# Filled stacks handed to two cross-attention layers, and keys projected ahead of queries

## The reference

```
q = split_heads(layernorm(x) @ w_q + b_q)        # 8 batches, 256 queries, 16 heads of 8
k = split_heads(ctx @ w_k + b_k)                 # 512 keys; ctx is 8 x 512 x 128
v = split_heads(ctx @ w_v + b_v)
scores = einsum('bhqd,bhkd->bhqk', q, k) / sqrt(8)
scores = where(mask == 0, -inf, scores)          # L3x only
x = x + merge(softmax(scores) @ v) @ w_o + b_o   # biases in L1x and L3x only
```

## Time and profile before

| | |
|---|---|
| median of 3 runs | 2776.68 us (2775.05 to 2780.43) |
| the profiled execution | 2782.93 us |
| its span | 2781.1 us, 48541 instructions |
| TensorE busy | 2335.9 us (84%) |
| VectorE busy | 1546.6 us (56%) |
| ScalarE busy | 1362.9 us (49%) |
| GpSimd busy | 728.6 us (26%) |
| mean granted clock of TensorE | 0.921 of 2.4 GHz |

### The profile page before, as it was taken

How to read it: one execution, slowest core, us unless ns; L and a number is a source line. 1 busy time by engine, 2 the same in 40 slices (tenths; PEclk the granted TensorE clock), 3 DMA queues, 4 the chain that set the end, 5 groups by cost and what they waited for, 6 DMA issues and landing times. The chain is left out here.

```text
span 2781.1 us, 48541 instructions
## 1 busy us (share of the span) xinstructions
PE 2335.9 (84%) x16549; PEld 1490.2 (54%) x16595; DVE 1546.6 (56%) x4593; ACT 1362.9 (49%) x3631; POOL 728.6 (26%) x1007
## 2 busy tenths in 40 slices
PE   6969998778898499953759999876969998799989
PEld 4634444745555144431646766555947776366653
DVE  4757772146666677733026666462447776677730
ACT  3736662135554266644217677431326655455542
POOL 0123212444434323102542232114421111322100
PEclk9979999979999699976779999997979999899999
DMA  2023225120000233230440000243520000332200
GB/s 78 2 77 94 86 61 177 37 76 31 25 23 16 57 101 93 65 97 15 93 85 1 2 2 1 80 90 104 162 72 2 1 2 11 99 81 82 61 18 15
DMA packets 129748, 158.29 MB, mean 57 GB/s; under 512 B 23121, under 2 KB 92122, under 8 KB 128355
## 3 DMA queue, kind: packets, MB, share of 16 engines
q1 hardware_dynamic: 117220, 143.47, 18.1%
q0 software_dynamic: 9664, 10.41, 1.8%
q10 hardware_dynamic: 2624, 1.32, 0.3%
HBM read 119.28 MB, written 36.56 MB: 56 GB/s over the span
## 5 line engine op out<-in xcount | busy, mean ns | idle before, releaser
L542 ACT ACTIVATE L3x_p_ring<-L3x_ps_t 128x512 f32<-128x512 f32 x256 | 142.0, 598 | 114.6 <-PE L3x_ps_t L622 113.8
L438 DVE CUSTOM_DVE_ANT_0 L3x_ps_s<-L3x_ps_s,L3x_mask_q 128x512 f32<-128x512 f32 x256 | 169.9, 718 | 38.1 <-PE L3x_ps_s L601 37.0
L542 ACT ACTIVATE L1x_p_ring<-L1x_ps_t 128x512 f32<-128x512 f32 x256 | 140.5, 619 | 87.7 <-PE L1x_ps_t L620 87.7
L441 DVE TENSOR_REDUCE L0x_mx<-L0x_ps_s 128x2 f32<-128x1024 f32 x128 | 152.3, 1221 | 40.3 <-PE L0x_ps_s L601 39.1
L542 ACT ACTIVATE L0x_p_ring<-L0x_ps_t 128x512 f32<-128x512 f32 x256 | 140.8, 622 | 66.8 <-PE L0x_ps_t L620 66.8
L441 DVE TENSOR_REDUCE L1x_mx<-L1x_ps_s 128x2 f32<-128x1024 f32 x128 | 152.2, 1221 | 30.5 <-PE L1x_ps_s L601 29.5
L965 ACT ACTIVATE L2a_probs<-L2a_ps_s,L2a_top 128x256 f32<-128x256 f32 x256 | 117.8, 472 | 78.9 <-DVE L2a_top L915 78.9
L965 ACT ACTIVATE L3a_probs<-L3a_ps_s,L3a_top 128x128 f32<-128x128 f32 (+1 forms) x256 | 104.0, 422 | 39.3 <-DVE L3a_top L911 37.2
L620 PE MATMUL L3x_ps_t<-L3x_q_stack,L3x_k_stack 128*128 128x256 bf16 x512 | 120.6, 275 | 2.7 <-DMA L3x_q_stack<-L3x_m_rows 2.4
L622 PE MATMUL L3x_ps_t<-L3x_mask_k,const_ident_bf 128*128 128x256 bf16 x512 | 119.9, 273 | 0.0
L620 PE MATMUL L0x_ps_t<-L0x_q_stack,L0x_k_stack 128*128 128x256 bf16 x512 | 86.4, 278 | 9.3 <-DMA L0x_q_stack<-L0x_m_rows 3.8
(11 more groups left out here) (718 smaller groups left out, 6204.9 us busy)
## 6 DMA issues: line engine op xcount, KB each, us to landing
L2f_w_e<-L2f_in_w_e SPq DMA_DIRECT2D x23, 544.0 KB
L0x_k_stack<-L0x_k_dram SPq DMA_DIRECT2D x96, 96.0 KB
L1x_k_stack<-L1x_k_dram SPq DMA_DIRECT2D x96, 96.0 KB
L3x_k_stack<-L3x_k_dram SPq DMA_DIRECT2D x96, 96.0 KB
L0f_w<-L0f_in_w SPq DMA_DIRECT2D x32, 256.0 KB, 5.3
L1a_rk_wide<-L1a_rk_dram SPq DMA_DIRECT2D x8, 1024.0 KB, 4.7
L1f_w<-L1f_in_w SPq DMA_DIRECT2D x32, 256.0 KB
kept_x<-ctxT SPq DMA_DIRECT2D x24, 256.0 KB, 3.7
```

Of the source, the lines that this page charges most:

```text
L438: last = dve.tensor_tensor_reduce(span, span, mask_q[:, t, :], 1.0, 2 * MASKED, ALU.add, ALU.max, accum_out=mx[:, t, k:k + 1])
L441: last = dve.tensor_reduce(mx[:, :, k], s_bank(o), AX, ALU.max)
L542: act.activation(p_ring[:, u % RING, j * BANK:(j + 1) * BANK], t_bank(o), ACT.Exp, scale=scale).then_inc(out["t"].sem, 1)
```

## The change

The constants that no layer reads are gone, and the one that `keep_clock` reads has 4 rows instead of 16. For L0x and L3x the stacks are tiles of the surrounding program: GpSimd fills them whole with four memsets, in the first block for L0x and at `x` of batch 2 in L3a for L3x. L1x still has stacks of its own, which ScalarE fills in another order. In all three layers keys come ahead of queries: `k` and the key split move from -13 to -17 (slot 15, two turns before the batch's own), the split is two steps, and the first keys are split by VectorE, the first queries by GpSimd, which clears `v` after that. SyncE stores keys at -17 and queries at -14, loads each quarter's keys ahead of its queries, and leaves the queries of batch 0 to ScalarE's queue. The context load at `ln` (-19) stays where it was.

```
+def fill_stacks(pool, stacks, filled):
+    for n, word in (("k", ONE_PAIR), ("q", 0.0)):
+        for par in range(2):
+            pool.memset(stacks[n][:, par].rearrange("p h k -> p (h k)").bitcast(F32), word).then_inc(filled, 1)
...
-    for kind, k, time, phase in (("ln", 0, -19, 1), ("ln_rest", 0, -18, 1), ("x", 0, -16, 3), ("q", 0, -14, 2), ("k", 0, -13, 2),
-                                 ("split", 0, -13, 3), ("stack", 0, -7, 3), ("stack", 1, -6, 3), ("stack", 2, -5, 3),
+    for kind, k, time, phase in (("ln", 0, -19, 1), ("ln_rest", 0, -18, 1), ("k", 0, -17, 2), ("split_k", 0, -17, 3), ("x", 0, -16, 3),
+                                 ("q", 0, -14, 2), ("split_q", 0, -14, 3), ("stack", 0, -7, 3), ("stack", 1, -6, 3), ("stack", 2, -5, 3),
...
+        def load_stack(eng, name, quarter, b):
+            heads = slice(QUARTER * quarter, QUARTER * (quarter + 1))
+            stack, dram, stored, count = (q_stack, q_dram, q_stored, 32) if name == "q" else (k_stack, k_dram, k_stored, 16)
+            wait_tally(eng, stored, b, count)
+            for a in range(3):
+                rows = dram[a:a + 3] if name == "q" else dram[:]
+                eng.dma_start(stack[24 * a:24 * a + 24, b % 2, heads], rows.rearrange("i (d h) k -> (i d) h k", h=H)[:, heads]
+                              ).then_inc(stacked[quarter].sem, 16)
...
             def _(sp):
-                    if kind == "split":
+                    if kind == "split_k":
+                        wait_tally(sp, k_split, b, 4)
+                        sp.dma_start(k_dram[:].rearrange("i p k -> p i k"), parts["k"][:]).then_inc(k_stored.sem, 16)
+                    if kind == "split_q":
                         wait_tally(sp, q_split, b, 4)
...
-                        elif k == 0:
-                            sp.wait_ge(filled, 2 * (b + 1))
+                        elif clear_own and k == 0:
+                            sp.wait_ge(filled, 1 if b == 0 else 4)
+                        load_stack(sp, "k", k, b)
+                        if b > 0:
+                            load_stack(sp, "q", k, b)
...
             def _(pool):
-                            pool.memset(v[:], 1.0).then_inc(cleared, 1)
...
-                    if kind == "split":
+                    if kind == "split_k" and b > 0:
                         for quarter in stacked:
                             wait_tally(pool, quarter, b, 0)
                         wait_out(pool, ("k", 0, b))
                         split(pool, "k", k_split, b)
+                    if kind == "split_q":
+                        for quarter in stacked:
+                            wait_tally(pool, quarter, b, 0)
+                        wait_out(pool, ("q", 0, b))
+                        split(pool, "q", q_split, b)
+                        if b == 0:
+                            pool.memset(v[:], 1.0).then_inc(cleared, 1)
...
             def _(act):
+                if clear_own:
+                    act.wait_ge(two_made, 1)
+                    fill("k", 0)
...
+                    if kind == "split_q" and b == 0 and clear_own:
+                        fill("q", 0)
+                    if kind == "stack" and b == 0:
+                        if clear_own and k == 0:
+                            act.wait_ge(filled, 2)
+                        load_stack(act, "q", k, b)
+                        if clear_own and k == QUARTER - 1:
+                            fill("k", 1)
+                            fill("q", 1)
...
 def attention_rows(...):
             def _(pool):
+                    if kind == "x" and b == 2 and stacks is not None:
+                        fill_stacks(pool, stacks, filled)
...
 def keep_clock(pe, const, bank, times):
-    wide = const["max_rows"][:, 0:4, :].rearrange("p a k -> p (a k)")
+    wide = const["some_rows"][:].rearrange("p a k -> p (a k)")
...
 def load_constants(nc, const, x_sb, x, const_in, follow, stacks):
+            @block.gpsimd
+            def _(pool):
+                fill_stacks(pool, stacks, filled)
...
-BF16_CONSTS=('ident_bf','causal_min','max_rows','causal_q','causal_k','expert_rows','before','ones_bf')
+BF16_CONSTS=('ident_bf','causal_min','some_rows','expert_rows','before','ones_bf')
```

More of the change, by code:

```diff
@@ L490, in _, with fill @@
             def _(act):
[L491 to L498, removed]
+                def fill(name, par):
+                    rows = stacks[name][P // 2:P, par].rearrange("p h k -> p (h k)").bitcast(F32)
+                    words = two_ones if name == "k" else const["zero"]
+                    act.activation(rows, words[P // 2:P, 0:1].broadcast_to(list(rows.shape)), ACT.Copy).then_inc(filled, 1)
+                if clear_own:
+                    act.wait_ge(two_made, 1)
+                    fill("k", 0)
                 for o in order:
@@ L521, in _ @@
                         wait_tally(act, k_split, b, 0)
+                        if b == 0:
+                            ahead.loaded(act)
                         if qk_bias:
@@ L658, in attention_cross, with attention_rows @@
         sem.clear()
-def attention_rows(nc, x_sb, const, w, cfg, ahead, follow):
+def attention_rows(nc, x_sb, const, w, cfg, ahead, follow, stacks):
     C, kd = cfg["chunks"], cfg["kd"]
@@ L3372, in attention_fidelity_layer, with load_constants @@
         fidelity_tail(nc, x_sb, y_all, const, tail, name + "tail_")
-def load_constants(nc, ctx, x_sb, x, const_in, follow):
-    const = {n: ctx.enter_context(nc.sbuf_tensor("const_" + n, list(a.shape), BF16 if n in BF16_CONSTS else F32))
-             for n, a in const_in.items()}
+def load_constants(nc, const, x_sb, x, const_in, follow, stacks):
     with ExitStack() as own:
         sem = Semaphores(nc, own, "start_")
-        loaded, rounded = sem("loaded"), sem("rounded")
+        loaded, rounded, filled = sem("loaded"), sem("rounded"), sem("filled")
         wide = {n: own.enter_context(nc.sbuf_tensor("wide_" + n, list(const_in[n].shape), F32)) for n in BF16_CONSTS}
@@ L3426, in decoder @@
                 ahead[name].own = False
-        const = load_constants(nc, ctx, x_sb, x, const_in, follow.get("constants"))
+        const = {n: ctx.enter_context(nc.sbuf_tensor("const_" + n, list(a.shape), BF16 if n in BF16_CONSTS else F32))
+                 for n, a in const_in.items()}
+        room, stacks = ExitStack(), {}
+        stacks["L0x"] = cross_stacks(nc, room, "L0x_")
+        load_constants(nc, const, x_sb, x, const_in, follow.get("constants"), stacks["L0x"])
         pool_dma = lambda n: ctx.enter_context(nc.semaphore(n))
@@ L3440, in decoder @@
             elif name in ROWS:
-                attention_rows(nc, x_sb, const, layers[name], dict(ROWS[name], name=name + "_"), ahead[name], follow.get(name))
-            else:
-                attention_cross(nc, x_sb, const, layers[name], dict(ATTENTIONS[name], name=name + "_"), ahead[name])
+                if name == "L3a":
+                    stacks["L3x"] = cross_stacks(nc, room, "L3x_")
+                attention_rows(nc, x_sb, const, layers[name], dict(ROWS[name], name=name + "_"), ahead[name], follow.get(name),
+                               stacks.get("L3x") if name == "L3a" else None)
+            else:
+                attention_cross(nc, x_sb, const, layers[name], dict(ATTENTIONS[name], name=name + "_"), ahead[name], stacks.get(name))
+                room.close()
         if ORDER[-1] == "L3f":
@@ L3462, in consts @@
     c['minus_half']=np.full((128,16),-0.5,np.float32)
-    c['head_rows']=(i[:,None]//8==np.arange(16)[None]).astype(np.float32)
-    mr=np.zeros((128,16,128),np.float32)
+    some_rows=np.zeros((128,4,128),np.float32)
     for p in range(3):
[L3466 to L3470, removed]
+        for h in range(4): some_rows[16*p+h,h]=1
+    c['some_rows']=some_rows
+    later=np.where(i[None,:]>i[:,None],np.float32(1e30),np.float32(0))
+    c['causal_min']=np.concatenate([np.zeros((128,128),np.float32),later],1)
     c['rank_down']=np.broadcast_to((32-np.arange(32)).astype(np.float32),(128,32)).copy()
```

56 lines of the change are left out of this document (20 added, 36 removed).

## The result

The changed kernel took 2837.09 us (median of 5 runs, 2833.02 to 2842.55) against 2775.74 of the kernel before on the same chip: a ratio of 1.0218, 95% interval 1.0201 to 1.0236. It is slower by 61 us. The profiled execution took 2836.67 us (span 2834.5), 53.7 more than that of the kernel before (2782.93, which lay above its median).

What follows compares the result with a forecast made beforehand. TensorE's program order was taken to bound the steady part. Gains -19.5, fill +8.5, waits +38 and clock +9 gave +36 us: 2818.9 against the profiled execution, 2812.7 against the median; range 2782 to 2843.

Steps and rivals of the forecast that it cites:

- Constants: Before the first layer: about 0.9 MB less to load, taken as -2 us, at most 4.4 us gained.
- Starts of L0x, L1x, L3x: Cross layers' starts: earlier key stores and first scores; -8.5 us in L0x, -2 in L1x, -7 in L3x.
- The sentence about query loads: Start of L0x: twelve key loads issued ahead would delay query loads by perhaps 2 us, making the part worth -6.5.
- Fill in L3a: At x of batch 2, GpSimd's memsets delay VectorE's xn and TensorE: +8.5 us (4.4 to 13), half clock included.
- Waits of the key matmul: Cross layers from batch 2 on: the key matmul waits for the late context load, 18 waits, +38 us.
- Half clock: After waits over 2 us TensorE runs at half clock: +9 us at half of ten waits, 0 to 17.
- Keys ahead of queries: Cross layers: the key matmul moves to slot 15 of the turn before and waits for the context tile: +38 us.
- the first (free waits): Cross layers: slack in the batch absorbs TensorE's wait, sum -11 us, 2765.7 us; chance 0.10.
- The second (maxima rows behind the key store): L0x and L1x: maxima's rows wait behind SyncE's key store, 1.6 us in 12 batches, +19, 2785 us; chance 0.08.

Runs made afterwards that it cites:

- the two runs: Queries first, spread fill, filler matmuls ahead of the wait for clearing v: first batch's query loads on ScalarE's queue, 2759.5 us; on SyncE's, 2760.8 us.
- The spread fill: The changed kernel with L3a's four memsets put singly into GpSimd's longest gaps instead of in a row: 2820.4 us.
- the early load: The changed kernel with SyncE issuing the context load at -27 instead of -19, ahead of maxima rows and stack loads: 2791.8 us, ratio 1.0057.
- The held split: The changed kernel with the context load issued early, and GpSimd's key split also waiting for VectorE's maxima parts of batch b-2: 2781.1 us, ratio 1.0019.
- the rows ahead of the stacks: Keys first with early context load, held key split, spread fill, earlier filler, query loads on SyncE, maxima rows issued before next batch's stack loads: 2778.6 us, ratio 1.0009.

## Why the prediction was right, and where it was not

Direction and mechanism hold; 2837.1 lies in the range, 24 us above the forecast. The sum was made against the profiled execution of before, so its terms are compared there: +36 forecast, +53.7 measured.

- *Constants*: -2 forecast, -2.4 measured (first layer begins at 21.6 instead of 24.0).
- *Starts of L0x, L1x, L3x*: -8.5, -2 and -7 forecast; by first `t` against the layer's start -7.2, -4.0 and -7.9. The sum is near (-17.5 and -19.1), the way there was not: first scores in L0x gained 2.1 us, not 6.2, since filler matmuls behind the clearing of `v`, and the query loads with them, took the rest (with both out of the way they came 6.8 earlier than before, 14.2 us after the start); the way from there to first `t` gained 5.2, not 2.3. The sentence about query loads held up 2 us behind the key loads was near the mark: 2.4 to 3.4. The Trainium skill (DMA: Bandwidth & Descriptors, Rules for kernel authors) has all issuing engines share the same 16 DMA engines, so that a second one brings no bandwidth; the two runs agree (143 GB/s with two, from 163 to 168 us, and 170 with one, from 160 to 165). Here the second queue even cost time; whether by itself, or because the key loads of later quarters no longer stood behind the first queries, was not told apart.
- *Fill in L3a*: +8.5 forecast, +11.9 measured. This term was mis-sized: memsets and the two halves of `xn` were taken to alternate (6.5 us). The first half took 10.33 us, the second ended with it, and all four memsets passed: TensorE idled for 9.3, near the bound of 10, and 2.7 went to the half clock, where 2 had been taken. The spread fill shows that the place made the price.
- *Waits of the key matmul*: +38 in 18 forecast, +35.9 in 17 measured; the early load takes them to none. SyncE's queue was the cause, as stated.
- *Half clock*: +9 forecast; from first `t` to the layer's end, busy time times one minus the granted clock grew by 5.9 in L0x and 3.2 in L1x and fell by 0.3 in L3x, in all 8.8.
- *What was missing*: +14.3, the waits for the maxima's parts. The step that failed is the part "Keys ahead of queries", which moves the key matmul and prices only its wait. GpSimd's split moves with it, to the moment when VectorE makes the parts. The earlier trace rows had shown a VectorE instruction held by a memset, and the prediction used this for the fill alone. The held split shows the cause. Of this the Trainium skill (SBUF — State Buffer, Who interferes with whom) says that a VectorE instruction with two SBUF inputs contends with a GpSimd instruction that reads SBUF; the trace agrees (1.13 us instead of 0.17).
- *The rest*: the terms add up to +49.4; the other +4.3 lies spread over steps that were not told apart, and is less than an untouched layer moves from run to run (L1a, above).

Of the rivals, the first (free waits) is out: from first `t` to the end L0x grew by 28.8 us, and its waits and half clock account for some 27, so a batch gave nothing back. The second (maxima rows behind the key store) was rightly priced at nothing while the key matmul waits; once that wait is gone it costs 6 us more than in the changed kernel, and 27 with the rows ahead of the stacks (29.0 in all against 2.1). The median rose by 61 us, the profiled execution by 53.7, because the profiled execution of before lay 7 us above the median of these runs (2775.74) and that of after at its own.

## What to carry to other kernels

When a step is moved forward, list what it needs and where each need's issue stands in its queue, and list what every engine does at the new moment: here the load that had not moved cost some 45 us and the split that had moved with it another 11. Background work on GpSimd has a price that depends on what VectorE is about to do, so put each piece behind an instruction that starts a long gap, not in front of a step that the bound engine waits for. In a start-up, take away one limit at a time and look at what is late next: earlier scores brought nothing until the maxima's rows had left the queue of the next batch's loads.

## What the runs showed of the hardware that was not expected

- VectorE's `xn` was held through four memsets in a row, 10.33 us, without getting in between them. Between the instructions of GpSimd's split, each of which waits for the one before, VectorE did get in: at 268.85 a step took its usual 0.18 us, and the steps that were held were held for one split instruction at a time, up to 1.14 us.
- Steps as small as 16 columns can be held to the end of the GpSimd instruction that started before them: 0.17 us became 1.13 beside one of 1.18.
- Twelve loads on a second queue, issued from 1.6 us after the first of twelve on another, let the first scores, which wait for the first quarter, start 7.1 us after their first issue (160.82 to 167.94); in one queue, in the order of need, it was 3.7 (159.78 to 163.49).
